# Two layers of attention and experts: GpSimd's clearing, context blocks, mean subtraction, key parts and masks put at other times, v cleared by VectorE

## The reference, cut to what matters

```python
x = x + mlstm(layernorm(x), ctx, ctx, ...)        # block 0: 4 heads of 32, gates, cumulative sums, decay
x = x + experts16(layernorm(x), ...)              # block 1: 16 experts, top 4, and a shared one; silu
x = x + attention(layernorm(x), ctx, ctx, ...)    # block 2: 16 heads of 8, softmax
x = x + experts8(layernorm(x), ...)               # block 3: 8 experts, top 2; gelu

# block 0, per head: cs = cumsum(log_sigmoid(fg)); log_D = cs_i - cs_shift_j + ig_j, causal
# D = exp(log_D - max); C = (q k / sqrt(32)) * D; h = C v / max(|sum C|, exp(-max)); per-head norm of h
# block 2: Q = xn Wq + bq, K = ctx Wk + bk, V = ctx Wv + bv; softmax(Q K / sqrt(8)) V Wo + bo
```

## Time and profile before

| | us |
|---|---|
| median of 3 runs | 284.03 |
| lowest, highest | 283.59, 285.62 |
| profiled execution, its own time | 285.0 |
| profiled execution, span | 283.2 |
| busy: PE, DVE, ACT, POOL | 231.7, 207.9, 164.4, 117.1 |

### The profile page before, as it was taken

The page is one execution under the profiler, slowest core; times in us unless marked ns, Lnnn a source line. Parts: engine busy times, 40 slices in busy tenths (PEclk is TensorE's granted clock), DMA queues, the critical chain, the costliest instruction groups (busy, mean ns, idle before and its releaser), DMA issues.

```text
span 283.2 us, 6143 instructions
## 1 busy us (share of the span) xinstructions
PE 231.7 (82%) x2136; PEld 152.5 (54%) x2136; DVE 207.9 (73%) x519; ACT 164.4 (58%) x281; POOL 117.1 (41%) x144
## 2 busy tenths in 40 slices
PE   8569892787899996875957529969999999999993
PEld 3225690353555554452746427546666667766673
DVE  3978659894788888789799966656666676667674
ACT  1040347869444445058777826255777877888781
POOL 1989162385464640486353540020165345345000
PEclk9999996868799999796597969977999999999999
DMA  6801410001011103022000000000003120100002
GB/s 248 328 0 30 94 30 0 0 28 29 3 55 31 56 0 148 0 67 84 0 2 1 2 0 3 0 0 3 0 6 104 43 79 14 61 0 0 2 2 74
DMA packets 6648, 11.53 MB, mean 41 GB/s; under 512 B 1120, under 2 KB 4320, under 8 KB 6496
## 3 DMA queue, kind: packets, MB, share of 16 engines
q1 hardware_dynamic: 5520, 10.35, 11.5%
q10 hardware_dynamic: 1104, 0.87, 0.9%
HBM read 9.64 MB, written 0.52 MB: 36 GB/s over the span
## 4 chain that ended last, share of the span: by engine, by line
PE 47%; DVE 24%; issue 14%; ACT 6%; POOL 4%; DMA 2%; DVEq 1%; SPq 0%; ACTq 0%; POOLq 0%
PE ps L1304 5%; PE ps L1306 5%; PE ps L1305 5%; DVE xn L654 4%; PE ps L1292 4%; PE ps L1291 4%; PE ps L1290 4%; DVE xr L991 3%; PE ps L1169 2%; PE ps L1171 2%; DMA pk<-pack 2%; PE ps L1170 2%; DVE attention_or_experts L854 2%; POOL rstd L320 2%; DVE keys_or_scores L863 2%
## 5 line engine op out<-in xcount | busy, mean ns | idle before, releaser
L980 DVE SCALAR_TENSOR_TENSOR attention_or_experts<-ps,attention_or_experts 128x512 f16<-128x512 f32 x64 | 43.2, 687 | 26.1 <-ACT attention_or_experts L608 25.8
L1304 PE MATMUL ps<-wsp,attention_or_experts 128*128 128x128 f16 x256 | 47.2, 222 | 2.6 <-DVE xr L991 1.6
L603 ACT ACTIVATE ps<-ps 128x512 f32<-128x512 f32 x64 | 37.3, 583 | 19.7 <-PE ps L1292 19.7
L1306 PE MATMUL ps<-wsp,attention_or_experts 128*128 128x128 f16 x256 | 47.2, 222 | 0.0
L1305 PE MATMUL ps<-wsp,attention_or_experts 128*128 128x128 f16 x256 | 47.2, 222 | 0.0
L608 ACT ACTIVATE attention_or_experts<-ps 128x512 f16<-128x512 f32 x64 | 37.8, 592 | 0.0
L1022 PE MATMUL ps<-idle 128*128 128x512 f16 x100 | 27.4, 433 | 8.0 <-ACT v L485 5.4
L1304 PEld LDWEIGHTS ps<-wsp,attention_or_experts 128*128 128x128 f16 x256 | 25.4, 99 | 15.1 <-issue 5.4
L1305 PEld LDWEIGHTS ps<-wsp,attention_or_experts 128*128 128x128 f16 x256 | 25.5, 99 | 5.9 <-issue 0.6
L404 POOL TENSOR_SCALAR wsp<-raw 128x512 f16<-128x512 f32 x16 | 9.9, 618 | 43.3 <-PE ps L1292 31.7
L320 POOL TENSOR_TENSOR rstd<-ve,minus_half 128x4 f32<-128x4 f32 x8 | 8.1, 1017 | 46.9 <-DVE ve L647 46.9
(11 more groups left out here) (194 smaller groups left out, 581.6 us busy)
## 6 DMA issues: line engine op xcount, KB each, us to landing
raw<-w_second SPq DMA_DIRECT2D x8, 512.0 KB, 3.8
raw<-w_first SPq DMA_DIRECT2D x9, 192.0 KB, 2.3
attention_or_experts<-ctx_v SPq DMA_DIRECT2D x1, 1056.0 KB, 9.7
rw<-rows ACTq DMA_DIRECT2D x1, 512.0 KB, 6.5
ctxT<-ctx_t SPq DMA_DIRECT2D x1, 512.0 KB, 7.1
kS<-xhi SPq DMA_DIRECT2D x8, 64.0 KB, 2.2
kS<-xlo SPq DMA_DIRECT2D x8, 64.0 KB, 2.0
out<-xr SPq DMA_DIRECT2D x2, 256.0 KB, 2.3
```

What stands on the lines that cost most here:

```text
L603: a.activation(bank(k % 4), bank(k % 4), ACT.Gelu, scale=1 / (XS * XS)).then_inc(s["gelu"], 1)
L980: v.scalar_tensor_tensor(hlo[:, k % 4, :], bank(k % 4), HS, hhi[:, k % 4, :], ALU.mult, ALU.subtract)\
L1304: mm(o, hhi[:, k % 4, ts], wsp[:, p, 0, cs], start=(c == 0 and t == 0), stop=False, skip_group_check=True)
L1306: last = mm(o, hlo[:, k % 4, ts], wsp[:, p, 0, cs], start=False, stop=(c == FC - 1), skip_group_check=True)
```

## The change

- GpSimd's first work is now the clearing of ctxM, then combt and log_ps, and only then rsqrt(0, g).
- v1 and its constant columns are cleared by VectorE, at its start, before the statistics.
- The scaling of the context blocks waits for xn_ready of both groups.
- The mean subtraction of v0 comes before khi and klo, and waits for cm_ready.
- The five key masks and wqr move behind the splits of pairs 2 to 7 of block 1.
- Split 0 comes right behind klo, before rsqrt(1, g); split 1 waits until xn_ready is 2 G. The splits of block 3's first experts wait until it is 3 G.

```diff
--- before.py
+++ after.py
@@ -325,44 +325,32 @@
                     .then_inc(s["kM_ready"], 1)
 
             fill(pool.memset(minus_half[:], -0.5))
-            for g in range(G):
-                rsqrt(0, g)
-            pool.wait_ge(s["rstd_ready"], G)
-            pool.memset(log_ps[:], math.log(PS))
+            pool.memset(ctxM[:], 0.0).then_inc(s["ctxm_zero"], 1)
             fill(pool.memset(combt[:], 0.0))
             pool.memset(combt[:, :, :, X0:X0 + 1], XS).then_inc(s["comb_zero"], 1)
-            pool.memset(ctxM[:], 0.0).then_inc(s["ctxm_zero"], 1)
-            fill(pool.memset(v1[:], 0.0))
-
-            pool.memset(v1[0:S, :, :, 8:9], VS)
-            pool.memset(v1[S:P, :, :, 17:18], VS).then_inc(s["v1_zero"], 1)
-            pool.wait_ge(s["v1_zero"], 1)
+            pool.memset(log_ps[:], math.log(PS))
+            for g in range(G):
+                rsqrt(0, g)
 
             pool.wait_ge(s["in_ctx"], 16)
             pool.wait_ge(s["ctxm_zero"], 1)
+            pool.wait_ge(s["xn_ready"], G)
             for h in range(H0):
                 q = slice(h * D0, (h + 1) * D0)
                 pool.tensor_scalar(ctxM[q, :, h, :], ctxT[q, :].rearrange("p (b s) -> p b s", s=S), D0 ** -0.5, 1.0,
                                    ALU.mult, ALU.mult).then_inc(s["ctxm_ready"], 1)
                 pool.wait_ge(s["ctxm_ready"], h + 1)
 
+            pool.wait_ge(s["cm_ready"], 1)
+            pool.wait_ge(s["vmean_ready"], 1)
+            v0g = v0[:].rearrange("p b c (h d) -> p (b c h) d", h=2)[:, :, 0:D0]
+            pool.tensor_tensor(v0g, v0g, vmean[:].unsqueeze(2).to_broadcast([P, NB * 4, D0]), ALU.subtract).then_inc(s["v0_ready"], 1)
+
             pool.wait_ge(s["kT_ready"], G)
             pool.tensor_scalar(khi[:], kT[:], 1.0, 1.0, ALU.mult, ALU.mult).then_inc(s["khi_ready"], 1)
             pool.wait_ge(s["khi_ready"], 1)
             pool.tensor_tensor(klo[:], kT[:], khi[:], ALU.subtract).then_inc(s["klo_ready"], 1)
-            pool.wait_ge(s["in_qkvo"], 16)
-            pool.tensor_scalar(wqr[:].rearrange("p j (r f) -> p j r f", f=32),
-                               wq[:, 0, :].rearrange("p (j f) -> p j f", f=32).unsqueeze(2).to_broadcast([P, 4, 4, 32]),
-                               AS, 1.0, ALU.mult, ALU.mult).then_inc(s["wqr_ready"], 1)
-
-            pool.wait_ge(s["vmean_ready"], 1)
-            v0g = v0[:].rearrange("p b c (h d) -> p (b c h) d", h=2)[:, :, 0:D0]
-            pool.tensor_tensor(v0g, v0g, vmean[:].unsqueeze(2).to_broadcast([P, NB * 4, D0]), ALU.subtract).then_inc(s["v0_ready"], 1)
-            pool.wait_ge(s["kS_ready"], 16 * 16)
-            for h in range(5):
-                key_mask(h)
-            for g in range(G):
-                rsqrt(1, g)
+            pool.wait_ge(s["klo_ready"], 1)
 
             def split_pair(j, p, arrivals):
 
@@ -380,13 +368,24 @@
                     pool.tensor_tensor(wsp[:, p, 1, c], raws[:, c], wsp[:, p, 0, c], ALU.subtract).then_inc(s["wsp_ready"], 1)
 
             split_pair(0, 0, 16)
+            for g in range(G):
+                rsqrt(1, g)
+            pool.wait_ge(s["xn_ready"], 2 * G)
             split_pair(1, 1, 16)
 
             pool.wait_ge(s["v1hi_ready"], 1)
             pool.wait_ge(s["comb_ready"], G)
             pool.tensor_tensor(v1lo[:], v1[:], v1hi[:], ALU.subtract).then_inc(s["v1lo_ready"], 1)
+            pool.wait_ge(s["in_qkvo"], 16)
+            pool.wait_ge(s["kS_ready"], 16 * 16)
             for j in range(2, PAIRS):
                 split_pair(j, j % 2, 16 * (j // 2 + 1))
+                if j < 7:
+                    key_mask(j - 2)
+                if j == 7:
+                    pool.tensor_scalar(wqr[:].rearrange("p j (r f) -> p j r f", f=32),
+                                       wq[:, 0, :].rearrange("p (j f) -> p j f", f=32).unsqueeze(2).to_broadcast([P, 4, 4, 32]),
+                                       AS, 1.0, ALU.mult, ALU.mult).then_inc(s["wqr_ready"], 1)
             for g in range(G):
                 rsqrt(2, g)
 
@@ -407,6 +406,7 @@
                     pool.tensor_tensor(wsp[:, p, 1, c], raws[:, c], wsp[:, p, 0, c], ALU.subtract).then_inc(s["wsp1_ready"], 1)
 
             pool.wait_ge(s["mm2"], 2 * PAIRS)
+            pool.wait_ge(s["xn_ready"], 3 * G)
             split_expert(0, 0, 16)
             split_expert(1, 1, 16)
 
@@ -656,6 +656,9 @@
                 last.then_inc(s["xn_ready"], 1)
 
             v.memset(idle[:], 0.0).then_inc(s["idle_set"], 1)
+            stat(v.memset(v1[:], 0.0))
+            v.memset(v1[0:S, :, :, 8:9], VS)
+            v.memset(v1[S:P, :, :, 17:18], VS).then_inc(s["v1_zero"], 1)
 
             for g in range(G):
                 v.wait_ge(in_x[g], 16)
```

More of the change, by code:

```diff
@@ L327, in _ @@
             fill(pool.memset(minus_half[:], -0.5))
+            pool.memset(ctxM[:], 0.0).then_inc(s["ctxm_zero"], 1)
+            fill(pool.memset(combt[:], 0.0))
+            pool.memset(combt[:, :, :, X0:X0 + 1], XS).then_inc(s["comb_zero"], 1)
+            pool.memset(log_ps[:], math.log(PS))
             for g in range(G):
                 rsqrt(0, g)
-            pool.wait_ge(s["rstd_ready"], G)
-            pool.memset(log_ps[:], math.log(PS))
-            fill(pool.memset(combt[:], 0.0))
-            pool.memset(combt[:, :, :, X0:X0 + 1], XS).then_inc(s["comb_zero"], 1)
-            pool.memset(ctxM[:], 0.0).then_inc(s["ctxm_zero"], 1)
-            fill(pool.memset(v1[:], 0.0))
-            pool.memset(v1[0:S, :, :, 8:9], VS)
-            pool.memset(v1[S:P, :, :, 17:18], VS).then_inc(s["v1_zero"], 1)
-            pool.wait_ge(s["v1_zero"], 1)
             pool.wait_ge(s["in_ctx"], 16)
             pool.wait_ge(s["ctxm_zero"], 1)
+            pool.wait_ge(s["xn_ready"], G)
             for h in range(H0):
```

## The result

| | before | after |
|---|---|---|
| median, us (four executions each, in turn on one chip) | 284.82 | 275.15 |
| all executions | 283.59 to 286.64 | 274.70, 274.76, 275.54, 278.70 |
| profiled execution: own time, span | 285.0, 283.2 | 274.7, 272.9 |
| TensorE's mean granted clock in it | 0.916 | 0.937 |

The ratio is 0.9693, 95% interval [0.9636, 0.975]: faster by some 3%.

A forecast was written before the change was run, and what follows sets the result against it. VectorE's SBUF operations, standing still beside GpSimd's, were taken as the bound. Gains of 3.0, 0.5, 2.7, 0.54, 0 and 0.1, say 6.8, off the profiled 285.0 gave 278.2, a median of 277.2 us; range 274.5 to 281.0.

The forecast's parts named there:

- the rival of the clock: TensorE's clock, 0.50 at 59 to 60 us in the router, may stay full with shorter PE gaps: 275.0; chance 0.12.
- Part 1: The start: L654 runs without GpSimd beside it, L676 starts at about 15.35 instead of 18.33: 3.0 us.
- Part 2: The rows from L676 to L689: with GpSimd silent, PE's long chain (L1084) starts another 0.5 us earlier.
- The rest of the scan's gain ends there: Beyond PE's earlier start, the cumulative maximum's gain is hidden, since the cmax transposes stand behind two groups of PE work.
- Part 3: The head chain: without the five masks beside it, VectorE's small operations shorten, 2.7 us in series.
- Part 4: The second normalization: L654 at 55.40 falls from 1.66 beside the first split to 1.12: 0.54 us.
- Part 5: The first experts: masks and wqr behind the splits of pairs 2 to 7 cost 0, bounds 0 to 0.5 a pair.
- Part 6: The second attention: L654 gains 1.45 gross, VectorE's chain about 0.6, 0.5 given back: 0.1 taken.
- Rival two: TensorE's clock stays full in the router and first pairs because PE's gaps shrink: 275.0; chance 0.12.
- v's clearing isn't held: Answers the smaller-gain rival: at the start GpSimd's clearing holds VectorE's clearing of v, total 279.9; chance 0.18.
- GpSimd doesn't bound the first experts: Answers the slower rival: masks and split pieces stretch, six pairs cost 2 us each, total 289; chance 0.04.
- the operations do shorten: Answers the no-effect rival: VectorE's stretched operations are slow by themselves, only the order shifts, total 284; chance 0.06.

The follow-up runs named there:

- the start alone: Kernel before with only GpSimd's new first order, v cleared by VectorE and the scaling waiting for xn: 279.19 us, ratio 0.9803.
- masks with v0's wait: Kernel before with the five key masks and wqr moved and v0's subtraction waiting for cm_ready: 282.68 us, ratio 0.9907.
- the waits for xn: Kernel after without its two late waits for xn_ready (before split 1, before block 3's first experts): 276.78 us, ratio 0.9703.
- the masks alone: Kernel before with only the five key masks and wqr moved behind the splits of pairs 2 to 7: 285.80 us, ratio 1.0035.
- the rows undone: Kernel after with v0's subtraction put back behind khi and klo, without its wait for cm_ready: 277.06 us, ratio 0.9737.

## Why the prediction was right

Predicted 277.2 (274.5 to 281.0), measured 275.15. Against its own profiled execution the sum was 6.8 and the profile shows 10.3. The forecast's own range, 275.7 to 279, was missed; the wide one held because it took in the rival of the clock, and that the clock helped was luck, as it helped elsewhere than this rival said. The mechanism held. By its steps:

- **Part 1, 3.0: measured 3.91.** The mechanism held. v's clearing took 1.98, not 2.55, and with its two columns ended at 4.23, just ahead of the statistics at 4.28. The limit was the one named, vmean's multiplication behind the scaling; only its time was off: 14.42, not 15.35. The mis-sized term is the end of the second xn group, put at 10.8 and measured at 9.75, which starts the scaling 0.85 earlier. The statistics had come 0.28 earlier than before (x's load), and the eight L654 went in one run from 7.62. v0's load landed at 11.8, not 12.4, and PE's gates at 14.36, not 15.0: neither would have let the gates be read much sooner.
- **Part 2, 0.5: measured 0.37,** in the place named. But its worth inside the whole change is 1.1, by undoing it alone: without it v0's subtraction slides beside L689. The step "The rest of the scan's gain ends there" was costed against the old order, in which wqr keeps the subtraction away from L689.
- **Part 3, 2.7: measured 2.69.** ScalarE's masks start at 41.18, right behind its copies of v (48.16 in the earlier trace rows), and don't wait for kS.
- **Part 4, 0.54: measured 0.58.**
- **Part 5, 0: measured 0** for the masks (1.12 each, as costed). The 0.52 of this stretch isn't theirs, and no cause is shown. PE was granted 0.81 at 110 to 115 before, but that comes too late: its last products of the first experts start at 112.61 before and 104.55 after, already 8.06 apart. Of the 0.52, 0.33 arises in one pair, where VectorE's L806 stood still for 0.25 before and PE for 0.26 behind it.
- **Part 6, 0.1: measured 0.20, for the wrong reason.** "VectorE's chain gains only about 0.6" is wrong: the whole 1.45 arrives at the first maximum. Then 1.25 is given back until block 3. L844 takes 0.92 and 1.27 (1.14 and 0.81 before) beside remainders that are now at other places; the first maximum is 9.52 earlier, the last 9.50, the last tile's sum 8.77, rsqrt(3, 0) 8.70. Most of the loss thus comes behind the last maximum. There VectorE's sum waits 0.65 for PE, which was granted 0.50 from 148 to 152; at the same place before it was granted 1.00 (156 to 162), and VectorE didn't wait. So 0.8 of the 1.25 goes with the clock. The other 0.43, ahead of rsqrt(3, 1), has no cause shown.
- **The clock.** Rival two gave 275.0, which is where the time fell, but not by its mechanism: as in the earlier trace rows, the router is at 0.50 after too (stretches of the kernel after, columns as above):

```profile
51.00:52.00 1.00, 1.00 (x7) 1.00 (x6) 0.98 (x1) 0.47 (x2) 1.00 (x1) 0.50 0.00 0
```

What came instead are 2.0 at the start of block 3, less the 0.8 of part 6. So the forecast's places give 7.8 in these profiles (3.91 + 0.37 + 2.69 + 0.58 + 0.2), 2.0 is clock, and the 0.5 of the first experts is open.
- **The other rivals fell.** v's clearing isn't held; GpSimd doesn't bound the first experts; the operations do shorten.

The parts add up roughly once the slide is avoided: the start alone 5.5, masks with v0's wait 2.4, the waits for xn 1.3 to 1.6, sum 9.2 to 9.5; the change gives 9.6 where it was measured again (285.06 to 275.50). The intervals of the single parts are 2 to 5 us wide, so this sum is a weak witness; the landmarks of the profiles are the strong one.

Open: whether the start alone gives more than 3.9; why clearing v on GpSimd costs more in medians than in its profile; 0.4 of the 1.25 given back in block 2, and the 0.5 of the first experts; whether PE's gap at 16 us lets the clock fall; and how much of the miss with the masks alone was the clock in the executions that weren't profiled.

## What to carry to other kernels

Where VectorE's operations in SBUF are stretched, list what GpSimd runs beside them, and put GpSimd's reading work where VectorE reads PSUM or waits; a wait on VectorE's own semaphore does it, for 0.5 to 1.8 us each here. Taking an operation out of GpSimd's queue moves up all that stands behind it: look up what slides into the vacated place, and pin it with a wait. Here a slide cost 0.7 us of 2.7 in one kernel and 1.1 in another. And before a gain or a miss is explained by the order of the queues, compare the granted clock of the two profiles stretch by stretch: a fall of it that no edit touches cost 2.1 us here. A change that shortens the path also moves PE's idle gaps; filling one with products that nobody needs costs nothing where PE waits anyway.

## What the runs showed of the hardware that was not expected

- The same kernel on the same chip took 274.41 and 286.54 us. In the longer one TensorE's clock fell to 1.2 GHz at 20 us, behind an idle gap of 1.76 us, and stayed there for some 16 us of almost gapless work; that cost 8.2 us by the head chain. Another execution of a kernel with this start, behind a gap of 1.74 us, was granted 1.00 throughout that stretch.
- Two held operations ended 0.28 us after GpSimd's did: L690 at 31.45 against 31.17 with the masks alone, and L691 at 25.15 against 24.87 with the rows undone. (The scan L687 of before, 25.31 against 24.75 in the earlier trace rows, ended 0.56 after.)
- A VectorE clearing of 128x2304 took 1.98 us beside a GpSimd clearing, and GpSimd's of the same tile 2.02 to 2.16: both engines are about equally fast at it.
- GpSimd is held too. In the kernel after, its L363 at 49.61 and L365 at 50.88 take 1.31 and 1.37 us beside VectorE's two additions of the bias on v (L761, 49.43 to 51.98), which have two operands in SBUF; the same two operations took 0.40 each at 26.88 and 27.25.
